# Mask of the first layer: products of TensorE ahead of the scores, or an add of VectorE behind them

## The reference

```python
# layer 0
q, k, v = proj(Wq), proj(Wk), proj(Wv)            # 16 heads of 16
scores = einsum('bhsd,bhtd->bhst', q, k) * scale
scores = where(mask[None, None, :, :], -inf, scores)   # one 64x64 mask for all
out = einsum('bhst,bhtd->bhsd', softmax(scores), v) @ Wo.T
xn = out / rms(out) * rms_scale
x = x + xn * (1.0 + sc[:, None, :]) + shift[:, None, :]
# layer 1, no mask
y = x + attention(tc_rmsnorm(x, t, ...))
x = x + y + swiglu(tc_rmsnorm(y, t, ...))
```

## Time and profile before

| | |
|---|---|
| median of 3 runs | 346.4 us (344.65 to 347.71) |
| profiled execution | 349.28 us |
| its span in the profile | 347.5 us |
| PE busy | 331.4 us, 95%, 5444 instructions |
| PEld busy | 316.8 us, 91% |
| DVE busy | 219.1 us, 63%, 361 instructions |
| ACT busy | 214.7 us, 62% |
| POOL busy | 130.1 us, 37% |

### The profile page before, as it was taken

How to read it: one execution, slowest core, us unless ns; L and a number is a source line. 1 busy time by engine, 2 the same in 40 slices (tenths; PEclk the granted TensorE clock), 3 DMA queues, 4 the chain that set the end, 5 groups by cost and what they waited for, 6 DMA issues and landing times.

```text
span 347.5 us, 12627 instructions
## 1 busy us (share of the span) xinstructions
PE 331.4 (95%) x5444; PEld 316.8 (91%) x5444; DVE 219.1 (63%) x361; ACT 214.7 (62%) x462; POOL 130.1 (37%) x146
## 2 busy tenths in 40 slices
PE   4899879999999999999999999999999999999995
PEld 4787768899899999999999999999999999999994
DVE  1276984779875859584665738497495446547331
ACT  2488798889887856558556765556565337433221
POOL 3002369644535514531415212344453025135332
PEclk9999999999999999999999999999999999999999
DMA  7714854303012003000200100000000000100000
GB/s 177 214 32 122 239 199 125 122 13 115 4 45 83 3 2 93 2 2 32 70 27 2 33 3 4 2 2 32 4 2 32 5 2 0 32 2 2 32 30 30
DMA packets 11462, 17.11 MB, mean 49 GB/s; under 512 B 1552, under 2 KB 5648, under 8 KB 11408
## 3 DMA queue, kind: packets, MB, share of 16 engines
q1 hardware_dynamic: 11408, 16.31, 15.7%
HBM read 14.14 MB, written 2.16 MB: 47 GB/s over the span
## 4 chain that ended last, share of the span: by engine, by line
PE 90%; DVE 3%; DMA 2%; issue 1%; ACT 1%; SPq 1%; POOL 0%; ACTq 0%
PE ps L1430 65%; PE ps L1523 7%; PE ps L1537 6%; PE ps L1513 5%; DMA mask_u<-in_mask 2%; PE ps L1548 2%; PE ps L1569 2%; PE ps L1501 2%; DVE row_max L1041 1%; DVE probs L1049 1%; PE ps L1450 1%; ACT probs L600 1%; POOL h_lo L430 0%; ACT probs_T L607 0%; PE ps L1443 0%
## 5 line engine op out<-in xcount | busy, mean ns | idle before, releaser
L1430 PE MATMUL ps<-ff_hi,w_hi 128*128 128x256 f32 x256 | 74.3, 290 | 0.0
L1430 PE MATMUL ps<-ff_hi,w_lo 128*128 128x256 f32 x256 | 72.1, 282 | 0.0
L1430 PE MATMUL ps<-ff_lo,w_hi 128*128 128x256 f32 x256 | 72.1, 282 | 0.0
L430 POOL TENSOR_TENSOR h_lo<-w_stage,h_hi 128x512 fp32r<-128x512 f32 x32 | 41.2, 1288 | 72.6 <-ACT h_hi L660 72.5
L1041 DVE TENSOR_REDUCE row_max<-ps 128x8 f32<-128x512 f32 x64 | 43.7, 683 | 20.8 <-PE ps L1513 20.8
L1430 PEld LDWEIGHTS ps<-ff_hi,w_hi 128*128 128x128 f32 x256 | 48.2, 188 | 0.9 <-issue 0.7
L1430 PEld LDWEIGHTS ps<-ff_lo,w_hi 128*128 128x128 f32 x256 | 48.3, 189 | 0.0
L1430 PEld LDWEIGHTS ps<-ff_hi,w_lo 128*128 128x128 f32 x256 | 48.2, 188 | 0.0
L600 ACT ACTIVATE probs<-probs 128x512 f32<-128x512 f32 x64 | 39.8, 628 | 9.9 <-DVE probs L1049 9.5
L1049 DVE SCALAR_TENSOR_TENSOR probs<-row_max,ps 128x512 f32<-128x512 f32 x64 | 43.9, 686 | 1.9
L1430 PE MATMUL ps<-in_hi,w_hi 128*128 128x256 f32 x128 | 38.8, 303 | 5.5 <-DVE w_lo L1030 4.8
(11 more groups left out here) (90 smaller groups left out, 796.7 us busy)
## 6 DMA issues: line engine op xcount, KB each, us to landing
w_stage<-in_weights SPq DMA_DIRECT2D x20, 256.0 KB, 4.5
mod_tile<-mod_rows_dram SPq DMA_DIRECT2D x32, 128.0 KB, 3.0
x_T<-in_xT SPq DMA_DIRECT2D x8, 256.0 KB, 2.8
x_row<-in_x SPq DMA_DIRECT2D x8, 256.0 KB, 3.0
out<-x SPq DMA_DIRECT2D x8, 256.0 KB, 2.3
x<-in_cond SPq DMA_DIRECT2D x1, 392.0 KB, 6.5
x<-in_rows SPq DMA_DIRECT2D x1, 96.0 KB, 7.4
mod_rows_dram<-x SPq DMA_DIRECT2D x1, 64.0 KB, 1.6
```

Source lines behind the costliest of these rows:

```text
L430: pool.tensor_tensor(h_lo[q % 2][:], h_T[q % 2], h_hi[q % 2][:], ALU.subtract)\
L1430: mm = pe.matmul(dst, x, y, start=first and n == 0, stop=last and n == len(terms) - 1, skip_group_check=True)
```

## The change

The mask is no longer a product. `maximum` first adds `mask_neg` to the bank's scores on VectorE and writes the sum to the bank's `probs` buffer; in layer 0 the maximum and the shift then read that buffer in SBUF, and the shift writes it in place. In layer 1 both read PSUM as before. The scores' products now start their sums themselves. `sel_r` is gone, and `mask_neg` is float32. A semaphore `masked` counts the adds; the wait for a free `probs` buffer stands ahead of the add (and still ahead of the shift), the wait for the mask moves from TensorE to VectorE's first add, and `maximum` also waits for the shift of the same bank number of the chain before.

```diff
-        sel_r = sb("sel_r", [P, 2, S], F32R)
-        mask_neg = sb("mask_neg", [P, 2 * NR, S], F32R)
+        mask_neg = sb("mask_neg", [P, 2 * NR, S])
...
-                dve.tensor_tensor(sel_r[:], ident[:, 0:S].unsqueeze(1).to_broadcast([P, 2, S]),
-                                  ident[:, S:P].unsqueeze(1).to_broadcast([P, 2, S]), ALU.add).then_inc(sel_ready, 1)
...
             def maximum(a, r):
+                n, (c, l) = NR * a + r, CHAINS[a]
+                src = ps[:, S_BANK[a][r], :].rearrange("p (g s) -> p g s", s=S)
                 dve.wait_ge(scores_ready, a + 1)
-                dve.tensor_reduce(row_max[r][:], ps[:, S_BANK[a][r], :].rearrange("p (g s) -> p g s", s=S),
-                                  AX.X, ALU.max).then_inc(max_ready, 1)
+                wait(dve, shift_done, NR * (a - 1) + r + 1)
+                if l == 0:
+
+                    dst = probs[n % NPROB][:].rearrange("p (g s) -> p g s", s=S)
+                    if n == 0:
+                        dve.wait_ge(mask_ready, 1)
+                    wait(dve, pT_ready, n - NPROB + 1)
+                    dve.tensor_tensor(dst, src, mask_neg[:], ALU.add).then_inc(masked, 1)
+                    dve.wait_ge(masked, NR * c + r + 1)
+                    src = dst
+                dve.tensor_reduce(row_max[r][:], src, AX.X, ALU.max).then_inc(max_ready, 1)
 
             def shift(a, r):
 
-                n = NR * a + r
+                n, (c, l) = NR * a + r, CHAINS[a]
+                dst = probs[n % NPROB][:].rearrange("p (g s) -> p g s", s=S)
+                src = dst if l == 0 else ps[:, S_BANK[a][r], :].rearrange("p (g s) -> p g s", s=S)
                 dve.wait_ge(max_ready, n + 1)
                 wait(dve, pT_ready, n - NPROB + 1)
...
+                dve.scalar_tensor_tensor(out=dst, in0=row_max[r][:].unsqueeze(2).to_broadcast([P, 2 * NR, S]),
+                                         scalar=-BIG / 2, in1=src, op0=ALU.max, op1=ALU.subtract)\
+                    .then_inc(shift_done, 1)
...
             def scores(a, *readers):
-                c, l = CHAINS[a]
-                if a == 0:
-                    pe.wait_ge(mask_ready, 1)
-                    pe.wait_ge(sel_ready, 1)
                 bank_free(*readers)
-                if l == 0:
-
-                    for r in range(NR):
-                        rows = slice(S * (r % 2), S * (r % 2) + S)
-                        pe.matmul(ps[:, S_BANK[a][r], :], sel_r[rows].rearrange("q b s -> q (b s)"),
-                                  mask_neg[rows].rearrange("q g s -> q (g s)"),
-                                  start=True, stop=False, skip_group_check=True)
...
-                                               start=l == 1, stop=True, skip_group_check=True)
+                                               start=True, stop=True, skip_group_check=True)
```

More of the change, by code:

```diff
@@ L177, in build @@
         ident_ready, ones_set, roots_set = sem("ident_ready"), sem("ones_set"), sem("roots_set")
-        parity_ready, sel_ready, mask_ready = sem("parity_ready"), sem("sel_ready"), sem("mask_ready")
+        parity_ready, mask_ready, masked = sem("parity_ready"), sem("mask_ready"), sem("masked")
         cond_ready, silu_ready = sem("cond_ready"), sem("silu_ready")
```

## The result

| | before | after |
|---|---|---|
| median (runs) | 346.78 us (4) | 366.60 us (4) |
| lowest to highest | 344.65 to 347.71 | 365.87 to 367.87 |
| ratio, 95% interval | | 1.0584 (1.0526 to 1.0643) |
| profiled execution | 349.28 us | 366.91 us |
| its span | 347.5 us | 365.1 us |

The change costs 19.8 us. The sign of the forecast (357.9 us) was right; the size was not, and 366.6 us lies above its range (350.5 to 364). In the text behind this point "the stop" is a pause of TensorE in the scores of chain 7, which no wait explains; it turns out to be a fifth of the loss.

The account below looks back on a forecast made before the run. VectorE's chain of waits was taken to bound the first 54 us, TensorE's work the rest from about 60. Terms 7.6 + 2.1 + 2.05 + 0.45 + 0.6 - 1.3 = 11.5 on 346.4 gave 357.9 us, range 350.5 to 364.

Parts of the forecast that it names:

- the start: Chains 0 to 2, up to keys of chain 3: 7.6 us later, plus 2.1 us for shared access with GpSimd.
- products gone and sel_r: TensorE in layer 0: 0.67 us saved per chain where TensorE is last ready, and 0.20 us for sel_r.
- adds in chains 0 to 2, with shared access: VectorE's adds at 0.72 us a bank before keys of chain 3, plus 2.1 us for shifts meeting GpSimd.
- adds in chain 4, up to scores of chain 6: Scores of chain 5 wait for a late shift of chain 4's third bank: net +1.2 us instead of -0.67.
- adds in chain 6, up to hidden_in: Late shifts delay chain 5's values product and chain 6's last transposition: +2.05 us in all after chain 6.
- adds in chain 8, both stages up to scores of chain 10: Late shift of chain 8's second bank delays its transposition: +1.1 - 0.67 = +0.45 us.
- adds in chains 10 and 12: Adds there hide because readers come later and VectorE is 66% busy: -0.67 us each, -1.3 together.
- shared access, chains 4 to 8: Shifts reading two SBUF inputs beside GpSimd: 2.1 us more VectorE time, a third reaching a wait, 0.6 us.
- the waits that were named: TensorE waits near 2 us ahead of scores of chain 5 and 1.6 ahead of chain 5's values product.
- Shift of chain 0's last bank: Expected sign on VectorE in the start: this shift starts near 26.6 us, 2.0 us later than 24.57.
- Rival (e): TensorE's clock falls to 1.2 GHz during waits between 46 and 58 us: +3.5, 361.4 us, once more 365; chance 0.23.
- TensorE idle in 30 to 64 us grown by more than 8 us: Expected sign of a right forecast: TensorE's idle time between 30 and 64 us grows by over 8 us.

Follow-up runs that it names:

- k9: Kernel after with no mask in layer 0 and 20 more transpositions in the warm-up at the start: 343.08 us, ratio 0.988 to before.
- k8: Kernel after with 38 instead of 18 transpositions in the warm-up at the start: 362.62 us, ratio 1.046 to before.
- k12: Kernel before with 38 instead of 18 transpositions in the warm-up at the start: 348.05 us, ratio 1.005 to before.
- k1: Kernel after with the mask of layer 0 left out, neither products nor adds: 346.27 us, ratio 0.998 to before.
- k7: Kernel after with adds in chains 10 and 12 only and mask products in layer 0's other chains: 348.22 us, ratio 1.003 to before.
- k4: Kernel after with adds in chains 0 to 2 and mask products in chains 4, 6, 8, 10 and 12: 356.09 us, ratio 1.025 to before.
- k11: Kernel after with adds as separate steps and VectorE's steps of chains 0 to 2 reordered so dependent ones are rarely neighbours: 363.44 us, ratio 1.049 to before.
- k6: Kernel after with 72 filler transpositions of the identity in TensorE's waits of chains 0 to 2: 366.21 us, ratio 1.058 to before.
- k5: Kernel after with the add's sum written back into PSUM, where maximum and shift read it: 363.49 us, ratio 1.050 to before.

## Why the prediction was wrong

By the medians the 19.8 us split in three: products gone, k9 minus before, -3.7; adds, k8 minus k9, +19.5; the stop and what follows, after minus k8, +4.0. The stages give -4.1, +19.9 and +4.2. The 20 products more of k8 and k9 are in the first part; alone they cost 0.8 in the kernel before (k12). Against the forecast's steps, its credits and its adds taken apart (credits 0.87 + 5 x 0.67 = 4.2; so chain 4 is 1.2 + 0.67 = 1.9, chain 6 is 0.85 + 0.67, chain 8 is 0.45 + 0.67, the start 7.6 + 2.1 + 0.87), and the adds measured as k8 minus k9 in the table of stages:

| step | forecast, us | measured, us |
|---|---|---|
| products gone and sel_r | -4.2 where they count | -4.1 (before to k9) |
| adds in chains 0 to 2, with shared access | +10.6 | +11.1, of them some 1.2 a fall of the clock |
| adds in chain 4, up to scores of chain 6 | +1.9 | +2.5 |
| adds in chain 6, up to hidden_in | +1.5 | +2.5 |
| adds in chain 8, both stages up to scores of chain 10 | +1.1 | +0.1 + 1.4 |
| adds in chains 10 and 12 | 0 | +0.7 + 1.6 |
| shared access, chains 4 to 8 | +0.6 | within the rows above |
| the stop and what follows | no term | +4.2 (4.0 by the medians) |
| sum | +11.5 | +20.0 (19.8 by the medians) |

**The step that failed, first:** the prediction had no term for TensorE's own program. By the earlier trace rows, "there the end is set by how much TensorE has to do", and the products taken away were counted as 0.67 us a chain and nothing else. 20 products taken away ahead of one place moved the program under it, and the stop grew from 0.23 to 1.82 us there, with the clock at the 1.2 GHz level behind it. That the stop costs this much is shown by k8, k9 and k1: with 20 products put in at the start it is gone, and 4.0 us go with the adds, 3.2 without (4.2 and 4.4 by the stages). That it is the fetch of the program is argued: it rests on its place, the same product number in seven kernels, and on the packet 2.3 to 2.9 us ahead of each restart. What sets the time at which the packet is sent, 2.1 us ahead of its need before and 0.5 after, stays open, and with it why the stop is between 0 and 1.82 us long. The hint was in the trace of before: the pause of 0.23 us by "issue" in a step without a wait.

**The second:** "Behind chains 10 and 12 the readers come several products later and VectorE is 66% busy there: -0.67 each, -1.3". The adds there cost 2.3 us (k8 minus k9), 1.9 by k7 (its two stages, -0.16 + 0.76 = 0.6 above before, and the 1.33 of two chains' mask products that should have been saved). The step took a busy share for slack. It looked at the readers of the scores' banks and of the probabilities, as for chains 4 to 8, and not at what stands behind the adds in VectorE's list: the norm of the output before, and the low part of the output before.

**Sizes that were low by less:** chain 4 by 0.6 and chain 6 by 1.0; the waits that were named did appear there, 1.67 ahead of the scores of chain 5 (forecast near 2) and 1.22 ahead of its values product (1.6). What comes between is not known. The start was low by 0.5 with the fall of the clock in it, and high by 0.7 without.

**What was right.** The start: 10.2 us longer, where 9.7 and the 0.2 of sel_r were forecast, with the mechanism as told. How near the two numbers are is partly luck: k4, without the early fall of the clock, has 9.1. Shift of chain 0's last bank: 24.49, which is 8.84 behind the start of the scores (6.60 before): 2.24 more, where 2.88 - 0.67 = 2.2 was worked out. The time per add: 21.9 us for 32, and 0.72 us for a dependent start. k4 shows the start's loss alone, k11 that a part of it, 1.0 us against k4, are the latencies. The shared access was seen in the start, in two shifts and not three, 1.0 us against 2.1. **Rival (e)** was right that the clock would fall in the start, and wrong in its place and price: it named waits of 2 to 3 us between 46 and 58 us, and the longest there is 1.80. The fall whose price is known came earlier, at 26.2, and cost 1.2 us; filling the waits gave 0.8 (k6). The fall behind the stop cost about 1.2 us too. The expected sign "TensorE idle in 30 to 64 us grown by more than 8 us" failed for the same reason: it grew from 3.75 to 8.5 us, since slow products filled the rest.

The start's length varies by more than a microsecond with the falls of the clock in it: k4, which is the kernel after in this stretch, has 45.67, k8 47.17 and the kernel after 46.82, and the last two have the early fall.

## What to carry to other kernels

Work may go to an engine with a busy share of two thirds only after its own list was read around each new instruction: what stands behind it, and who waits for that. When instructions are taken out of a dense stretch of TensorE, look in the trace of before for pauses without a releaser, and after the change for the same pause moved: 20 instructions ahead of everything gave 4 us in the kernel after and cost 0.8 in the kernel before. To learn whether a lost gain was never there or went elsewhere, run the removal without the replacement (k1): it told in one run that the adds were not to blame for it.

## What the runs showed of the hardware

- TensorE stopped inside a step without waits, at the same product number in seven kernels, for 0.23 to 1.82 us, and went on 2.3 to 2.9 us behind a 16 KB packet of the instruction queue. Behind the stops of 1.82 us (after) and 1.47 (k1) the granted clock was at the 1.2 GHz level for 3.4 us, behind those of 1.27 (k5) and 1.59 (k6) it was not.
- One stretch of 3.4 us at the 1.2 GHz level made the start 1.2 us longer (after against k4).
- A shift with both inputs in SBUF took 1.15 and 1.26 us where it met an addition of GpSimd, 0.69 alone. A maximum that read SBUF beside the same addition took 0.69.
- The operations of VectorE on 128x512 took the same from SBUF as from PSUM: maximum 686 and 684 ns in the kernel after:

```profile
L1050 DVE TENSOR_REDUCE row_max<-ps 128x8 f32<-128x512 f32 x32 | 21.9, 684 | 12.8 <-PE ps L1510 12.8
```
